# Dividing attention outputs without transposing them: softmax sums by DMA in place of TensorE transposes

## What is computed

```python
a1 = _attn(q, k1, v1, causal=True)
a2 = _attn(q, ks, vs, causal=False)
a3 = _attn(q, kw, vw, causal=True)
out = g[:, 0] * a1 + g[:, 1] * a2 + g[:, 2] * a3
out = out.transpose(0, 2, 1, 3).reshape(B, T, N_HEAD * V_HEAD)
return out @ w_proj
```

## Time and profile before

| what | value |
|---|---|
| median of 3 runs | 3217.22 us (3217.02 to 3219.11) |
| the profiled execution | 3220.07 us, its span 3218.3 us |
| busy: PE / weight loads / DVE / ACT / POOL | 3080.5 / 2243.4 / 1979.1 / 1496.4 / 924.2 us |
| granted TensorE clock, mean | 0.979 of full speed |
| DMA | 16 GB/s on average |

### The profile page before, as it was taken

How to read it: one execution, slowest core, us unless ns; L and a number is a source line. 1 busy time by engine, 2 the same in 40 slices (tenths; PEclk the granted TensorE clock), 3 DMA queues, 4 the chain that set the end, 5 groups by cost and what they waited for, 6 DMA issues and landing times. The chain is left out here.

```text
span 3218.3 us, 58165 instructions
## 1 busy us (share of the span) xinstructions
PE 3080.5 (96%) x20368; PEld 2243.4 (70%) x20368; DVE 1979.1 (61%) x6929; ACT 1496.4 (46%) x3340; POOL 924.2 (29%) x1828
## 2 busy tenths in 40 slices
PE   4999899999999999999999999999999999999988
PEld 3777677767777677776777767776677767776655
DVE  4666556665566755766557656567556675565555
ACT  1544344454444534455444454444544455444444
POOL 0223223332333223332223322233222322223331
PEclk7999999999999999999999999999999999999999
DMA  3000000000000010000000000000010000000000
GB/s 115 21 14 14 21 14 21 14 1 27 14 27 8 1 34 14 21 8 8 27 14 21 8 8 27 20 21 1 7 34 21 14 1 14 21 21 1 1 1 14
DMA packets 34287, 55.97 MB, mean 17 GB/s; under 512 B 3536, under 2 KB 16592, under 8 KB 33744
## 3 DMA queue, kind: packets, MB, share of 16 engines
q1 hardware_dynamic: 34000, 52.26, 5.1%
HBM read 48.06 MB, written 4.19 MB: 16 GB/s over the span
## 5 line engine op out<-in xcount | busy, mean ns | idle before, releaser
L1642 ACT ACTIVATE PR<-work 128x512 f32<-128x512 f32 (+1 forms) x1088 | 638.4, 598 | 666.4 <-PE work L997 586.3
L1270 DVE CUSTOM_DVE_ANT_0 work<-work,KEEPB 128x128 f32<-128x128 f32 (+3 forms) x1536 | 667.1, 480 | 111.6 <-PE work L958 111.2
L1761 POOL TENSOR_SCALAR_AFFINE_SELECT PR<-PR 128x256 f32<-128x256 f32 (+1 forms) x960 | 351.0, 369 | 854.1 <-ACT PR L1642 848.0
L1251 DVE TENSOR_TENSOR BIG<-work,BIG 96x512 fp32r<-96x512 f32 (+1 forms) x448 | 278.2, 627 | 367.2 <-ACT BIG L1541 366.1
L958 PE MATMUL work<-BIG 96*128 96x448 f32 (+8 forms) x1664 | 449.2, 363 | 23.9 <-DVE X L1422 8.5
L995 PE MATMUL work<-BIG 99*128 99x512 f32 (+4 forms) x1152 | 416.2, 361 | 10.6 <-DVE BIG L1251 3.5
L1751 POOL TENSOR_TENSOR TOK<-AB 128x256 f32<-128x256 f32 (+1 forms) x320 | 216.0, 675 | 700.1 <-DVE AB L1221 694.7
L1039 PE MATMUL outs<-PR,ONES 128*32 128x512 f32 (+4 forms) x2304 | 404.8, 458 | 0.0
L958 PEld LDWEIGHTS work<-BIG 96*128 96x128 f32 (+1 forms) x1664 | 274.4, 197 | 159.7 <-issue 89.7
L996 PE MATMUL work<-BIG 96*128 96x512 f32 (+4 forms) x1152 | 382.2, 332 | 0.0
L997 PE MATMUL work<-BIG 96*128 96x512 f32 (+4 forms) x1152 | 380.6, 330 | 0.0
(11 more groups left out here) (163 smaller groups left out, 5094.6 us busy)
## 6 DMA issues: line engine op xcount, KB each, us to landing
WKW<-w_kw_dram SPq DMA_DIRECT2D x64, 256.0 KB, 2.6
WSEL<-w_sel_dram SPq DMA_DIRECT2D x64, 256.0 KB, 3.0
HN<-x_dram SPq DMA_DIRECT2D x8, 512.0 KB, 4.7
X<-x_dram SPq DMA_DIRECT2D x8, 512.0 KB, 4.6
out_dram<-X SPq DMA_DIRECT2D x7, 512.0 KB, 3.2
WFC<-w_fc_dram SPq DMA_DIRECT2D x1, 1024.0 KB, 9.9
WFP<-w_ffp_dram SPq DMA_DIRECT2D x1, 1024.0 KB, 11.8
WQKV<-w_qkv_dram SPq DMA_DIRECT2D x1, 768.0 KB, 13.3
```

The source lines that it names most:

```text
L1251: read_work(v.tensor_tensor(dst[1], src, dst[0].bitcast(F32), ALU.subtract), use)
L1270: last = v.tensor_tensor_reduce(ps[:, lo:hi], ps[:, lo:hi], KEEPB[:, T - (hi - lo):T], -1.0, -NEG, ALU.add, ALU.min, dst)
L1642: a.activation(PR[0:rows, j % NP, :], ps[0:rows, :], ACT.Exp).then_inc(exp_ready, 1)
L1761: gp.affine_select(blocks, blocks, [[0, len(cols)], [1, P]], ALU.is_ge, 0.0, base=0, channel_multiplier=-1).then_inc(exp_masked, 1)
```

## The change

Outputs stay as `values` leaves them. ACT copies a bank to `OE` and multiplies by the gate in the same instruction (the gate is 1.0 on the sum rows). SP then moves the sums by DMA: in layer 0, two DMAs take one partition each with its 3x512 sums and lay them on 24 partitions by 64 columns of `SUMS` (`gather`); in layer 1, four DMAs of 512 sums each. DVE inverts them all in one instruction (48x64 or 32x64). One DMA writes the inverses to DRAM (`PARK`), SP waits for it, and two DMAs (four in layer 1) read each head's inverses back to that head's 32 partitions (`spread_inverses`). DVE multiplies `OE` by them: three 64x512 products in place per pair in layer 0, one 128x512 product per group of four heads in layer 1, straight to `OT`. In layer 0 POOL adds three 64x512 tiles by two additions, the second to `OT`. All transposes of `out_tr` and `group` and the copies of `group_out` are gone. New steps `gather`, `recip`, `scale` and `sum` stand in the lists; those of a pass's last job stand in the next pass. The projection of layer 0 (`PROJ`) and the layer norm and first feed-forward half behind it move from a pass's end into the next pass, and so do the projection and the tail of layer 1 (`TAIL`). Many other numbers of the tables move a little.

```diff
-AFTER = [dict(pv=2.67, tr=2.03, sum=0.86, group=1.71, piece=-2.58, gap=0.66, piece_tr=2.36, max=4.98, max_gap=0.31, mt=1.78, rows=-5.38),
-         dict(pv=3.09, tr=1.94, group=2.19, max=-0.22, max_gap=1.03, mt=2.68, piece=32.75, gap=1.08, piece_tr=1.42)]
+AFTER = [dict(pv=2.67, recip=1.8, scale=3.2, late_recip=2.48, late_scale=5.5, scale_gap=0.82, last_recip=1.9, last_scale=3.81, piece=-2.58, gap=0.66, piece_tr=2.15, max=4.98, max_gap=0.31, mt=1.78, rows=-5.38),
+         dict(pv=3.17, recip=2.64, scale=5.15, last_recip=0.53, last_scale=4.91, max=-0.21, max_gap=1.03, mt=2.68, piece=32.73, gap=1.08, piece_tr=1.63)]
...
-PROJ = [("proj_early", 98.19), ("proj_last", 101.97), ("proj_add", 0, 102.07), ("proj_add", 1, 103.03),
-        ("var", 1, 0, 103.32), ("var", 1, 1, 103.48)]
+PROJ = [[("proj_early", 5.2), ("proj_last", 7.53), ("proj_add", 0, 7.63), ("proj_add", 1, 7.76),
+        ("var", 1, 0, 8.51), ("var", 1, 1, 8.75)],
...
+    def normalise(x, t0, t1):
+        at.append((t0, ("recip",) + x))
+        at.extend((t1 + AFTER[0]["scale_gap"] * i, ("scale",) + x + (i,)) for i in range(1 if x[0] else 3))
+        if x[0] == 0:
+            at.append((t1 + 2 * AFTER[0]["scale_gap"] + 0.01, ("sum",) + x))
...
+            def gather(layer, s, k):
+
+                j = job(layer, s, k)
+                if j >= 4:
+                    sp.wait_ge(parked, 16 * (j - 3))
+                sp.wait_ge(evacuated, OUT0[layer, s] + (3 if layer == 0 else 1) * (k + 1))
+                rows = JOB_ROWS[layer] * T // PIECE_W // JOB_DMAS[layer]
+                for i in range(JOB_DMAS[layer]):
...
+                    sp.dma_start(SUMS[rows * i:rows * (i + 1), j % 4, :], src).then_inc(gathered, 16)
+
+            def spread_inverses(layer, s, k):
...
+                sp.wait_ge(inverted, j + 1)
...
+                sp.dma_start(PARK[j % 4, 0:n].rearrange("(r k) -> r k", k=PIECE_W), sums_of(layer, j)).then_inc(parked, 16)
+                sp.wait_ge(parked, 16 * (j + 1))
...
+                for i in range(dmas):
+                    part = PARK[j % 4, n // dmas * i:n // dmas * (i + 1)].partition_broadcast(32)
...
+                    sp.dma_start(to, part).then_inc(spread, 16)
...
-            def transpose_tiles(use, src):
-                ps, done = take(use, W)
-                for t in range(NT):
-                    last = nc.tensor.transpose(ps[:, t * P:(t + 1) * P], src(t), ID[:, :])
-                last.then_inc(done, 1)
-
...
+            def invert(layer, s, k):
+
+                j = job(layer, s, k)
+                dve.wait_ge(gathered, job_dmas(layer, s, k))
+                v.reciprocal(sums_of(layer, j), sums_of(layer, j)).then_inc(inverted, 1)
+
+            def scale_attention(s, p, i):
+
+                if i == 0:
+                    dve.wait_ge(spread, job_dmas(0, s, p))
+                a = (A1, A3, A2)[i]
+                v.tensor_tensor(OE[0:64, a, :], OE[0:64, a, :], inverses(0, s, p)[:, a, :], ALU.mult).then_inc(weighted, 1)
+
+            def scale_heads(s, g):
+                dve.wait_ge(spread, job_dmas(1, s, g))
+                if g == 0:
+                    full(dve, ("proj", s + 1, 1) if s < B - 1 else ("sign", s - 1, 1), WORK)
+                v.tensor_tensor(OT[:, g, :], OE[:, g % 3, :], inverses(1, s, g), ALU.mult).then_inc(scaled1, 1)
...
-                    copy(OE[0][:, att, :], OB[att][:, :]).then_inc(evacuated, 1)
+                    if s + n:
+                        act.wait_ge(summed, NPAIR * s + n)
...
+                    g = 1 if att == A1 else 2 if att == A3 else 0
+                    a.activation(OE[:, att, :], OB[att][:, :], ACT.Copy, scale=GG[:, g:g + 1]).then_inc(evacuated, 1)
...
-            def group_out(s, layer, g):
-                ps = full(act, (s, layer, "group", g), WORK)
-                read_work(copy(OT[:, g, :], ps[:, :]), (s, layer, "group", g))
...
+                pool.wait_ge(weighted, 3 * (NPAIR * s + p) + 2)
+                in_order(gp.tensor_tensor(rows[A1], rows[A1], rows[A3], ALU.add))
+                pool.wait_ge(weighted, 3 * (NPAIR * s + p + 1))
+                gp.tensor_tensor(OT[64 * (p % 2):64 * (p % 2) + 64, p // 2, :], rows[A1], rows[A2],
                                  ALU.add).then_inc(summed, 1)
```

More of the change, by code:

```diff
@@ L250, in attention_steps @@
             for a in COMPLETE[layer].get(k, []):
-                if layer == 0:
-                    what, group = p, a == A2 and p % 2
-                elif p % 2:
-                    what, group = p // 2, True
-                else:
-                    continue
-                t1 = t + 0.3 + o["tr"]
-                at += [(t + 0.3, ("out", what, a)), (t1, ("out_tr", what, a)), (t1 + 0.1, ("norm", what, a))]
-                if layer == 0 and a == A2:
-                    at.append((t1 + 0.1 + o["sum"], ("sum", p)))
-                if group:
-                    at += [(t1 + o["group"], ("group", p // 2)), (t1 + o["group"] + 0.1, ("group_out", p // 2))]
+                what = p if layer == 0 else p // 2
+                if layer and p % 2 == 0:
+                    continue
+                at.append((t + 0.3, ("out", what, a)))
+                if layer or a == A2:
+                    at.append((t + 0.35, ("gather", what)))
+                    if what < JOBS[layer] - 1:
+                        late = "late_" if layer == 0 and what == JOBS[0] - 2 else ""
+                        t1 = t + 0.35 + o[late + "recip"]
+                        normalise((layer, s, what), t1, t1 + o[late + "scale"])
         b = n * (p - (1 if layer == 0 else 2))
@@ L281, in attention_steps @@
             at += [(o["rows"], ("rows", 0)), (o["rows"] + n, ("rows", 1))]
-        add(PROJ, s)
         if s > 1:
@@ L285, in attention_steps @@
         if s == 1:
+            add(PROJ[1], 0)
             add(MID_A[0], 0)
+            add([x[:-1] + (x[-1] + 7.0,) for x in MID_B], 0)
+        elif s:
+            add(MID_B, s - 1)
         if s:
-            add(MID_B, s - 1)
             add(HEADS[0], s - 1)
@@ L302, in attention_steps @@
         if s == B - 2:
-            add(MID_C, B - 1)
+            add([x[:-1] + (x[-1] + 13.0,) for x in MID_C], B - 1)
         if s == B - 1:
@@ L375, in attention @@
                     work.use((s, 0) + x + (h,))
-            elif what in ("unit", "max", "mt", "out_tr", "group"):
+            elif what in ("unit", "max", "mt"):
                 work.use((s, layer) + x, {"unit": 0, "mt": 2}.get(what, 1))
@@ L413, in plan_banks @@
     for x in TAIL_ORDER:
-        if x[0] == "wo":
-            work.end_kept((x[0], B - 1) + x[1:], x[1])
+        if x[0] == "wo_early":
+            for i in range(2):
+                work.hold(("wo", B - 1, i))
         elif x[0] == "tail_add":
-            work.held.discard(x[1])
+            work.held.discard(work.of["wo", B - 1, x[1]][0])
         elif x[0] in ("hT", "sign"):
@@ L1312, in attention @@
                         maxima(s, layer, x[1], x[2])
-                    elif x[0] == "norm":
-                        normalise(s, layer, x[1], x[2])
+                    elif x[0] == "recip":
+                        invert(*x[1:])
+                    elif x[0] == "scale" and x[1] == 0:
+                        scale_attention(*x[2:])
+                    elif x[0] == "scale":
+                        scale_heads(*x[2:4])
                     elif x[0] == "pro":
```

274 lines of the change are left out of this document (158 added, 116 removed), and 9 rows, old and new, of tables (MID_A, MID_C).

## The result

| | before | after |
|---|---|---|
| median | 3218.16 us (4 runs, 3217.02 to 3219.99) | 3161.95 us (4 runs, 3157.54 to 3162.29) |
| profiled execution, its span | 3220.07, 3218.3 us | 3157.54, 3155.8 us |
| PE busy, the rest of the span | 3080.5, 137.8 us | 2975.5, 180.3 us |

The ratio is 0.9822 (95% interval 0.9805 to 0.9839): 56 us faster, where 104 were forecast, and 7 us above the range of 3078 to 3155. Faster was right, the size was not.

A forecast was written before the change was run, and what follows sets the result against it. PE was taken as the bound: 3220.07 - 126 - 5 + 8 + 5 + 8 + 7 = 3117 us for the profiled execution, 3114 us against the median, 3.2% faster; range 3078 to 3155 us.

The forecast's parts named there:

- PE: what goes: On PE, 1152 transposes removed at 0.109 us each give 126 us, plus some 5 us of waits for banks.
- The lower bound of the text: On PE, removed transposes give about 100 us if those at the crossings, where DVE is the bound, give nothing.
- PE's idle time beyond the crossings: Sign of being wrong: if this grows, DVE's or ACT's order, not PE, sets the pace; no size given.
- The crossings and the chain: Layer crossings cost 8 and 5 us, the moved projection 8, the end 7; the DMA chain in steady state 0.
- The third term: Layer 0's projection leaves the DVE-bound crossing and costs PE the same later: 8 us given back (-36 to +24).
- The `recip` lines mostly do not wait: Sign on DVE that the reciprocals mostly find their gathered sums ready; no size given.
- DVE and ACT: DVE's load stays unchanged (+7 us, 1950 to 2050 us), hidden; ACT loses 38 us of copies, hidden under PE.
- POOL's longer additions: On POOL, 128 additions over 512 columns take 133 to 187 us for 94, hidden at 29% load.
- The crossings heal: Rival: at layer 0 to 1 crossings, PE's 4.5 us idle goes eight times; 3085 us, chance 0.17.
- DVE and POOL hold each other up: Rival: new DVE products reading SBUF twice collide with POOL, delaying masks; 3133 us, up to 3150, chance 0.12.
- The gather comes late: Rival: slow small DMAs delay DVE, then PE, in every pair; 3235 us, chance 0.04; mild form 3165 us, 0.07.
- The PE time saved is not real: Rival: something other than PE paces the units, so the time does not move; 3217 us, chance 0.02.

The follow-up runs named there:

- the version with gentler spacing: The change with sequence 0's MID_B shifted only at its beginning, plus MID_C pressed by 0.7 up to its last spike step; 3159.72 us, ratio 0.9811.

## Why the prediction was right or wrong

**"PE: what goes" failed, by size.** 126 us plus 5 us of bank waits were taken. Doubling the transposes gives 0.088 us each, and the change without its chain gained 0.086 each in the middle: about 100 us for all 1152. The distance of 0.109 us was read rightly and is no exception: in the trace of the kernel before, the groups of transposes hold PE's weight loads for 133 us in all, 0.116 each. What failed is the step from there to the program's time, that all of it comes back. In the middle PE's busy time fell by 73.4 us, 0.102 a transpose, but its idle time rose by 18.8 us, 10.7 of them with the chain and 8.1 without it. Over the whole program PE's busy time fell by 105 us and not by 126. The lower bound of the text (about 100) came true, and its reason was partly right: it named the places where DVE is the bound, and the passes of layer 1, where the change put more on DVE, gave back 3.4 us for 160 transposes. But the transposes of layer 0 gave less than 0.109 too, 0.080 when doubled, and why is open. This step is some 30 of the 48 us missed.

**The moved steps failed, by being left out.** The prediction treated the move of layer 0's projection only where it recurs, and put nothing down for the first and the last sequence, where `MID_B` moved back by 7 units and `MID_C` by 13. In the kernel before, these places cost 11 and 15 us. In the change, 7 to 8 us of the first were recoverable. It also counted eight crossings from layer 0 to layer 1 and charged them alike; `PASSES` has seven, and the ends of pass (0,0), which is followed by (0,1), and of (0,7) are where the two moves lie. Its text named "PE's idle time beyond the crossings" as the sign of being wrong, and that is what grew: by 11.7 us in pass (1,6) and 8.6 behind it.

**The crossings and the chain held, in sum.** 8 + 5 + 8 + 7 = 28 us were charged. The chain costs 17 to 21 us by the run without it, for 8 + 5 + 7 = 20: 7.0 at the end for 7 forecast, and 1.5 us a sequence in the middle for 1.7. The third term (8 us) has no run of its own; in the middle the passes of layer 1 lost some 6 us beside the chain, and those of layer 0 gained 6 us more than the price by doubling (51.2 for 44.8), so in sum nothing of it shows there. "The `recip` lines mostly do not wait" was true of 64 of 96; the 80 us that the others waited cost PE about a quarter of that, by the whole chain's 17 to 21 us. The flights were wrong singly: 3.1 us for a read of 192 KB and 2.0 for 64 KB where I had taken 2.6, and a write of 8 or 12 KB takes 1.4 where I had taken 3.2. Write and reading back together are 4.5 us in layer 0, for 5.8. At the end, from the last value products to the last `OT`, 5.1 us became 11.1 instead of 12.6:

```profile
3124.85 0.60 ACT L1632 ACTIVATE NRM<-outs 128x512 f32<-128x512 f32 x1 [1.58 <-PE outs L1146]
3126.20 2.65 SPq L792 DMA_DIRECT2D NRM<-NRM  x4
...
3129.92 0.54 DVE L1372 RECIPROCAL NRM<-NRM 32x64 f32<-32x64 f32 x1 [1.58 <-DMA NRM<-NRM]
3130.49 0.31 SPq L802 DMA_DIRECT2D park<-NRM  x1
3131.87 1.70 SPq L826 DMA_DIRECT2D HT<-park  x4
3135.24 0.69 DVE L1385 TENSOR_TENSOR OT<-NRM,HT 128x512 f32<-128x512 f32 x1 [4.78 <-DMA HT<-park]
```

Four gather issues hold SP for 2.65 us (0.66 each, not 0.33), and the gather stands behind the reading back of the group before; the write is quicker than assumed. The Trainium skill's page "DMA: Bandwidth & Descriptors" (anatomy of one DMA) puts the fixed cost at about 2.0 us, for the GpSimd path; the 64 KB reads, which SP issued, agree with that, the small writes lie below it at 1.4, and the end as a whole came out between its sum and mine.

**DVE and ACT held, POOL nearly.** DVE's load is 1960.8 us for 1950 to 2050. POOL's longer additions were taken as hidden; cutting one of the two gave 4 to 8 us, so they cost a little.

**The rivals.** *The crossings heal* fell: in 27 us around the first crossing PE is idle 5.2 us, for 4.5 before. *DVE and POOL hold each other up*: its time (3133 to 3150) is the nearest below the result, and its mechanism is there but tiny. The new products have a median under 750 ns:

```profile
L1379 DVE TENSOR_TENSOR NRM<-NRM x168: 670/676/1389, 136.8 to 2905.7; 64x512 f32<-64x512 f32 x168
```

Those that overlapped an instruction of POOL took 738 ns in the mean, the others 677. Single ones do reach 1389 ns, as the Trainium skill's page "SBUF — State Buffer" (who interferes with whom) would have it, but with a mean of 701 the cost is 0.025 us a product. *The gather comes late* in its mild form (3165 us, chance 0.07) hit the number (3161.95) by luck: the passes of layer 0 in the middle lose nothing to the chain. *The PE time saved is not real* fell with the 56 us.

**Does it close?** With the measured terms: -100 for the transposes, +21 for the chain, +26 for the places make -53 us, against -56 to -59 measured. By stretch, with the 7.5 us of the projection that crosses each cut: the last one should change by -15.5 + 6.7 + 16.7 + 7.5 = +15 us and changed by +14.7; the start by -22.5 + 3.2 + 10.8 - 7.5 = -16 us and changed by -22.6. So the loss at the end is accounted for, and the start did some 7 us better than its parts. The terms were measured in different surroundings (the places with transposes, the price at the old places), each is uncertain by about 5 us, and POOL's 4 to 8 us are not in the sum when the price is that of doubling. This is agreement and not a proof that they add up. What remains open is how the last stretch could be mended: the versions that shortened its gap were no faster, or slower.

## What to carry to other kernels

An instruction's distance to its neighbour in a burst was an upper bound here for what its removal gave back: 0.109 us against 0.02 to 0.09. Doubling the instruction in the kernel as it is prices it in one run, but not what moves into its place: in layer 1 that took nearly all of the gain. When a change moves a step to where its input comes later, follow everything behind it to the first and last turn of the loop: there the chain ends with nothing beside it, and a term that is nothing in the steady state was 15 us here. A wait that looks large in a list, such as DVE's 80 us for the gathers, costs only what the busiest engine then lacks; leaving the whole chain out showed 1.5 us a sequence in the middle.

## What the runs showed of the hardware

Removing and adding the same instructions were not worth the same: 0.055 us a piece for three of each four transposes taken out, 0.088 for as many again put in.

The same matmuls cost PE more at the lower level of its clock. In pass (1,6) the version with gentler spacing ran the same 561 matmuls as the change with a mean granted clock of 0.88 instead of 0.92, and PE's busy time was 116.28 us for 110.25, while its idle time was 22.6 us for 23.3. So the amount of idle time did not tell the clock, and in pass (0,1) it did not either: the change's windows from 510 and 530 us, with 2.1 and 1.7 us of idle time, had mean clocks of 0.88 and 0.95, but the one from 550 us, with 1.7 us too, had 1.00, and so had the 27 us with 4.5 us of idle time at the crossing before.

A DMA from one SBUF partition of 512 sums to a compact tile holds its queue for 0.66 us to issue, twice as long as a 256 KB load; in layer 0, with three times the sums, it is some 0.75 us.
